# Expert heads of a four-layer transformer kernel: the relative terms of four heads computed in one fill of four row tiles, in place of two fills of two

## The reference

```python
# experts of layer 4: H = 8 heads, E = 8 experts, P = 128
xv = jnp.einsum('bsd,hedp->bshep', x, v_w.reshape(H, E, D, P))
v = jnp.einsum('bshep,bshe->bhsp', xv, gate_v)
att = jax.nn.softmax(jnp.einsum('bhqp,bhkp->bhqk', q, k) * SCALE, axis=-1)
ctx = jnp.einsum('bhqk,bhkp->bqhp', att, v)
weighted = ctx[:, :, :, None, :] * gate_o[..., None]
out = jnp.einsum('bshep,hepd->bsd', weighted, o_w.reshape(H, E, P, D))
# attention of layer 4: 16 heads of 64, NB = 10 basis functions, 128 distances
R = (X @ Wr + br).reshape(b, t, h, nb).transpose(0, 2, 1, 3)
D_ntT = jnp.where(valid[None, :, :], b_nd[:, jnp.clip(d, 0, maxlen - 1)], 0.0)
extra = jnp.einsum('bhtn,ntp->bhtp', R, D_ntT)
logits = jnp.einsum('bhtd,bhpd->bhtp', Q, K) / math.sqrt(dq) + bias + extra
```

## Time and profile before

| | us |
|---|---|
| median of 3 runs | 2207.71 |
| the three runs | 2207.71, 2204.81, 2207.71 |
| the profiled execution, its own time | 2203.68 |
| its span from first to last instruction | 2201.9 |
| granted TensorE clock, mean over the span | 0.94 |

### The profile page before, as it was taken

The page is one execution under the profiler, slowest core; times in us unless marked ns, Lnnn a source line. Parts: engine busy times, 40 slices in busy tenths (PEclk is TensorE's granted clock), DMA queues, the critical chain, the costliest instruction groups (busy, mean ns, idle before and its releaser), DMA issues. The chain is left out here.

```text
span 2201.9 us, 31669 instructions
## 1 busy us (share of the span) xinstructions
PE 1924.9 (87%) x9697; PEld 1011.3 (46%) x9697; DVE 1522.3 (69%) x4803; ACT 979.7 (44%) x2286; POOL 562.9 (26%) x967
## 2 busy tenths in 40 slices
PE   5588898449999965888699999999999999999998
PEld 3222333326655533333444444444444444466666
DVE  6566775627677663778688878877887777865554
ACT  3266665214376643422143333333333333267776
POOL 3478621340044410112000000000000000077777
PEclk9689999669999986999899999999999999999999
DMA  8432220663021200000144344442222111434332
GB/s 295 120 45 30 28 61 1 265 158 64 22 42 41 41 6 28 1 0 0 46 106 97 96 106 119 109 100 81 63 71 64 58 58 51 132 118 136 122 117 86
DMA packets 140765, 175.13 MB, mean 80 GB/s; under 512 B 15236, under 2 KB 117802, under 8 KB 139960
## 3 DMA queue, kind: packets, MB, share of 16 engines
q1 hardware_dynamic: 130328, 149.37, 23.8%
q0 software_dynamic: 10272, 23.73, 5.0%
HBM read 118.58 MB, written 54.48 MB: 79 GB/s over the span
## 5 line engine op out<-in xcount | busy, mean ns | idle before, releaser
L2514 DVE SCALAR_TENSOR_TENSOR x<-f_m,f_gs,x 128x128 f32<-128x128 f32 x1024 | 349.8, 345 | 86.1 <-PE f_m L2347 81.0
L600 DVE TENSOR_REDUCE a_nmax<-a_s 128x1 f32<-128x512 f32 (+3 forms) x512 | 278.9, 585 | 138.8 <-PE a_s L414 81.2
L2514 DVE SCALAR_TENSOR_TENSOR f_val<-f_m,gate,f_val 128x128 f32<-128x128 f32 x896 | 305.8, 344 | 68.2 <-PE f_m L2347 63.2
L2100 POOL TENSOR_SCALAR a_lg<-a_lg,a_rinv 128x256 f32<-128x256 f32 (+1 forms) x256 | 210.8, 843 | 482.2 <-DVE a_rinv L2137 481.8
L2347 PE MATMUL f_m<-f_wv,xnT 128*128 128x512 f32 x512 | 262.6, 597 | 4.6 <-DVE f_val L2514 4.6
L2347 PE MATMUL f_m<-f_wo,f_oT 128*128 128x512 f32 x512 | 261.5, 595 | 2.2 <-DVE f_val L2514 1.1
L519 ACT ACTIVATE a_pT<-a_st 128x512 f32<-128x512 f32 (+3 forms) x512 | 228.6, 520 | 31.2 <-PE a_st L440 14.0
L414 PE MATMUL a_s<-t_kp,t_qp 96*128 96x512 bf16 (+3 forms) x512 | 166.7, 361 | 4.9 <-DVEq L584 4.3
L437 PE MATMUL a_st<-t_qp,t_kp 99*128 99x512 bf16 (+3 forms) x512 | 162.9, 353 | 1.7 <-ACT a_pT L519 1.7
L2347 PEld LDWEIGHTS f_m<-f_wo,f_oT 128*128 128x128 f32 x512 | 95.5, 190 | 127.1 <-issue 107.3
L526 ACT CAST t_qp<-a_m 3x512 bf16<-3x512 f32 x128 | 73.9, 577 | 137.0 <-PE a_m L425 136.8
(11 more groups left out here) (397 smaller groups left out, 3461.1 us busy)
## 6 DMA issues: line engine op xcount, KB each, us to landing
a_rel<-band SPq DMA_DIRECT2D x64, 512.0 KB, 4.5
band<-f_hole POOLq DMA_DIRECT2D x16, 1032.0 KB, 9.7
f_wv<-f_wv_in SPq DMA_DIRECT2D x32, 512.0 KB
f_wo<-f_wo_in SPq DMA_DIRECT2D x32, 512.0 KB, 3.5
band<-f_rows SPq DMA_DIRECT2D x64, 256.0 KB, 3.7
w_gate_up<-f_wgu_in SPq DMA_DIRECT2D x4, 1536.0 KB, 19.1
t_qp<-parts SPq DMA_DIRECT2D x192, 32.0 KB
t_kp<-parts SPq DMA_DIRECT2D x192, 32.0 KB
```

What stands on the lines that cost most here:

```text
L600: v.tensor_reduce(nmax[:, h % 4, qt:qt + 1], s_ps[(b * H * QT + u) % R][:, 0:n], AX.X, ALU.max, negate=True)\
L2100: last = pool.tensor_scalar(lg[:, g % 2, half, p, c0:c0 + n], lg[:, g % 2, half, p, c0:c0 + n], rinv[:, g % 2, p, qt:qt + 1], None, ALU.mult)
L2514: ins = v.scalar_tensor_tensor(out, ps[:, e * P:(e + 1) * P], gate, out, ALU.mult, ALU.add)
```

## The change: one list of four heads in place of two lists of two

```diff
     relative = {}
     for n in range(B * RG):
         relative[8 * n] = [("r", n)]
-        relative[8 * n + 3] = [("e", 4 * n), ("e", 4 * n + 1)]
-        relative[8 * n + 5] = [("e", 4 * n + 2), ("e", 4 * n + 3)]
+        relative[8 * n + 4] = [("e", 4 * n + i) for i in range(4)]
```

## The result

| | before | change |
|---|---|---|
| median of 4 runs, us | 2206.33 | 2251.09 |
| lowest to highest | 2204.81 to 2207.71 | 2243.89 to 2252.18 |
| profiled execution | 2203.68 | 2252.18 |
| its span | 2201.9 | 2250.4 |
| granted clock, mean over the span | 0.940 | 0.927 |

The change is slower, clear of the noise: ratio 1.0196, 95% interval 1.0173 to 1.0219, or 44.8 us between the medians and 48.5 between the profiled executions. The forecast was 2230 in a range of 2214 to 2245. The direction was right. The size was about half of what came, and the result lies above the range.

A forecast was written before the change was run, and what follows sets the result against it. TensorE was taken to bound the expert stage. Fill and wait changes gave +14.5 us at full clock, clock falls +10, so 2203.7 + 24.5 = 2228.2 for the profiled execution; forecast 2230 us, range 2214 to 2245.

The forecast's parts named there:

- What bounds the stage: Expert stage: TensorE, busy 766.93 of 770 us, sets the pace, so each microsecond it waits is added to the time.
- the forecast's own sign: The prediction counts as wrong if, among other signs, the expert stage does not grow by 14 to 42 us.
- The fill: One fill of four heads, run side by side on TensorE, costs 1.29 us; the two old fills cost 2.68 per group.
- The upper bound of 2.15: Cost of the new fill if no more than two heads run at once: 0.86 us above 1.29.
- The wait: Before each fill TensorE waits for VectorE to read y': 2.17 us without gate step, 2.45 with narrow, 2.75 with wide.
- ScalarE's copies: The four bank copies after the fill free banks for v, y, v', y' about in time; costed at nothing.
- rival 1: The clock never falls: 2218 for the profiled execution, 2218 to 2223 for a run; chance 0.22.
- n = 0 and n = 15: First and last groups: +2.3 us where VectorE waits for fill and scores, +0.6 us where only y and y' count.
- The clock: Granted clock drops to 0.50 after the new wait in 6 groups of 16, 1.7 us each: +10 us.
- Rival 2: Clock falls nearly every time (2245), or the four heads do not run side by side (2242); chance 0.14.
- Rival 3: Faster, if VectorE has read y' when TensorE comes: saves 1.39 us per group, up to 22 us, 2182; chance 0.03.

The follow-up runs named there:

- e5: The change with the fill of four heads moved into unit 8n + 5, between the third and fourth product with the values; 2186.93 us.
- e6: Fill inside the values' product as in e5, but with 28 matmuls in place of 16, the extra ones recomputing the same results; 2191.64 us.
- e1: The change plus two full float32 products, results unused, issued by TensorE during the wait before the fill; 2226.73 us.
- e10: The change plus one unused full product ahead of the wait, where e1 has two; standstill 1.3 us, then the fill; 2222.35 us.
- e3: The kernel before, its two fills kept, plus a TensorE wait at the end of unit 8n + 4 until v, y, v', y' are read; 2264.93 us.
- e2: The change with the fill of unit 8n + 4 split into two fills of two heads in the same place; 2254.77 us.
- e8: The change plus one full float32 product, result unused, between the wait and the fill; 2267.36 us.
- e4: The change with the scores of unit 8n + 5 issued ahead of the fill; 2236.64 us.
- e9: e5 plus one unused full product and a wait for all four banks' reads at the end of unit 8n + 4, no fill near; 2229.86 us.
- e7: Fill inside the values' product as in e5, but with 52 matmuls per fill, the extra ones recomputing the same results; 2220.75 us.

## Why the prediction was right or wrong

**What bounds the stage: right.** TensorE's waits became time, unit by unit, and a fill without a wait (e5) became a gain of the same kind. By the forecast's own sign the stage was to grow by 14 to 42 us; its 16 groups grew by 46.8.

**The fill: right.** "I take 1.29": 1.31 in e5, 1.17 from first to last record. The upper bound of 2.15 is out. The 3.07 times that the Trainium skill gives for four row tiles ("TensorE: Matmul & The Clock Gate", section "Measured speedup vs the span model") is not borne out for these products of 128 columns: 3.9 times in e6 against e5. The 4 us that the rule would have added are not there.

**The wait: right.** Forecast 2.17, 2.45 and 2.75; measured 2.15, 2.45 and 2.74. The group costs 3.53 without a gate step, 3.42 in unit 8n + 4 and 0.11 behind it, where 3.43 was forecast: of the 0.1 that every fill leaves behind, my 1.29 held only a part (2.68 / 2 is 1.34). Weight loads of v and y did wait for ScalarE's copies (8.5 us in all), which the forecast had named as a sign of being wrong, but units 8n + 5 did not grow by it, so the copies cost nothing, as forecast. Over 14 groups this is 13.2 against 6.0 + 2.9 + 2.7 = 11.6. The experiments confirm the place: with the clock held in n = 1 to 14 the change stands at 2226.73 (e1), or at 2222.35 with one fall (e10), where rival 1 had 2218 to 2223. The profiled execution of e1 is 22.5 us above that of before, 8.0 more than the forecast's 14.5 at full clock: 1.6 in n = 1 to 14, 2.0 in n = 0, 0.8 in n = 15, and 3.6 outside these groups, where the code is the same (6.8 us of low clock behind the last scores among them).

**n = 0 and n = 15: too small.** Forecast +2.3 and +0.6, measured +4.4 and +3.1. For n = 15 e1 parts the two: 1.4 without a fall, so 1.7 are its fall of 3.4 us. For n = 0 the rest stays open. The clock was low for 10.2 us there and for 3.4 before, but with 6.8 us of it e1 takes 4.3.

**The clock: the step that failed.** "I take 6 falls of 16", at 1.7 us each, "since the outcome in these three rows was one of three". It was ten of 14, and n = 0 and n = 15 besides, and the mean price was 2.6: 1.7 for the four falls of 3.4 us, 3.0 to 3.3 for the six of 6.8. So 26.1 us came in n = 1 to 14 where the whole stage had been given 10: 16.1 of the 24.0 us by which the profiled execution missed the forecast's sum. Three parts of the step were wrong:

- The chance was taken from three cases that were not alike. All three lie where VectorE sets the pace, with TensorE busy for less than half of 3.4 us; none was a standstill between stretches of full work. e3 shows what that does: ten of 14.
- The price came from the only fall in the rows. The bound "a fall in every group, 16 x 1.7 = 27" was meant as the upper one, and it was none, because a fall can last twice as long. In the change, in e2 and in e8 the 30 falls in n = 1 to 14 part cleanly: where the (last) fill itself lasted 1.5 us or more, that is, ran at least partly at the low clock, the fall lasted 6.8 (18 falls); where it lasted 1.38 or less it lasted 3.4 (12 falls). In e3, without a fill there, nine of ten lasted 3.4. But the tenth lasted 6.8, and so did one fall of e4 whose fill lasted 1.22. So a fill that the low clock stretches may keep it low; this is a pattern with exceptions, and no experiment set it.
- The outcome was taken as loose chances per group. Two kernels with the same full-clock schedule, the change and e2, fell in the same ten groups.

**The rivals.** Rival 2 had the right side of the answer and a part of its mechanism, the falls, with a chance of 0.14, and its 2245 is 7 short for the profiled execution. That its 27 us for the clock come near the 26.1 is luck: it had sixteen falls at 1.7 us, and there were ten at 2.6. Rival 1 is what e1 and e10 come near to. Rival 3, faster by up to 22 us where the wait is covered, is e5: 19.2 us between the medians, in another place of the program.

What stays open: which of the groups with the same wait falls. n = 5 waited 2.74 us in the change, as long as any of the 14, and kept its clock. The 14 groups are not 14 trials of their own, so a difference of one or two falls between kernels shows nothing. And how much a fill adds to a standstill: two fills around 1.00 us fell in ten groups (e2), one fill behind 1.30 in one (e10).

## What to carry to other kernels

A packed group of products that needs all the buffers of a ring at once waits for the last of them. Put it where those buffers have been read, here inside a product that has a bank of its own (2186.93 us), and not behind the product that filled the last one (2251.09): the same packing gains 19 us or loses 45. When a wait of two microseconds is added to an engine that never stood still, price the clock beside the wait. Between the medians, moving the fill from its place in e5 to that of e1, behind the wait, costs 39.8 us, and the clock that falls when TensorE stands idle in that wait 24.4 more (e1 to the change). The packing had saved 19.2. Unused products in the gap bought the 24.4 back (e1).

## What the runs showed of the hardware that was not expected

- With full products on both sides, 2.2 us of standstill took the granted clock from 1.00 to 0.50 in ten groups of 14 (e3); 1.29 to 1.79 us took it in none of 22 (e9, e10). With a second wait of 0.64 us behind the fill, 1.30 us did in four groups of eight (e4).
- 1.00 us of standstill between two fills of ten-row matmuls went with the same falls as 2.15 us in front of one (e2 and the change, the same ten groups).
- A fall lasted 3.4 or 6.8 us, in n = 0 of the change 10.2.
- Records of ten rows and 128 columns on four row tiles came 3.9 and 3.8 times as fast as the 0.107 us each that one by one would take: 24 more in 0.66 us (e6), 72 more in 2.01 (e7).
